# Expert 2 and the output biases are loaded without waiting for the first gather, and the row limit of the indirect DMAs sits in one register

## The reference

```python
x = x + tanh(g_xattn) * (gelu(layernorm(x) @ ctx.T) @ ctx)          # per batch, ctx is 375 x 256
xf = layernorm(x).reshape(896, 256)
top1 = argmax(xf @ gate_w.T + gate_b)                                # 8 experts
y[t] = relu(xf[t] @ w1[top1[t]].T + b1[top1[t]]) @ w2[top1[t]].T + b2[top1[t]]
x = x + tanh(g_ffn) * y
```

## Time and profile before

| | us |
|---|---|
| median of 3 runs | 105.25 |
| lowest, highest | 104.97, 105.46 |
| the profiled execution | 105.14 |
| its span in the trace | 103.3 |
| PE busy | 95.3 (92%) |
| DVE, ACT, POOL busy | 51.8, 35.8, 39.6 |
| granted clock of PE, mean | 0.99 |

### The profile page before, as it was taken

How to read it: one execution, slowest core, us unless ns; L and a number is a source line. 1 busy time by engine, 2 the same in 40 slices (tenths; PEclk the granted TensorE clock), 3 DMA queues, 4 the chain that set the end, 5 groups by cost and what they waited for, 6 DMA issues and landing times.

```text
span 103.3 us, 2099 instructions
## 1 busy us (share of the span) xinstructions
PE 95.3 (92%) x676; PEld 88.2 (85%) x677; DVE 51.8 (50%) x203; ACT 35.8 (35%) x104; POOL 39.6 (38%) x96
## 2 busy tenths in 40 slices
PE   5999999999999799999999999999999999999700
PEld 5989988789978689999998898998998999988500
DVE  0643796767799758299584432350540431233100
ACT  5716458666684126333431140230230330400000
POOL 3448778333947507771025025730300300300330
PEclk9999999999999999999999999999999999999997
DMA  2999999999999501599999999999999310100110
GB/s 61 231 394 407 401 403 436 399 424 420 406 403 421 191 10 31 117 362 336 318 423 411 407 416 435 399 412 421 425 419 423 136 46 0 39 3 6 51 52 4
DMA packets 7086, 28.66 MB, mean 277 GB/s; under 512 B 1181, under 2 KB 2591, under 8 KB 5024
## 3 DMA queue, kind: packets, MB, share of 16 engines
q1 hardware_dynamic: 5040, 25.40, 61.7%
q0 software_dynamic: 864, 2.12, 6.7%
q10 hardware_dynamic: 1168, 0.98, 2.8%
HBM read 26.64 MB, written 2.11 MB: 278 GB/s over the span
## 4 chain that ended last, share of the span: by engine, by line
PE 85%; DVE 8%; issue 2%; POOL 1%; ACT 0%; POOLq 0%; DVEq 0%
PE bank L1069 24%; PE bank L1078 23%; PE bank L977 9%; PE bank L989 8%; PE bank L1085 5%; PE bank L1022 4%; PE bank L1032 4%; PE bank L967 2%; PE bank L1010 2%; PE bank L1056 1%; DVE x L642 1%; DVE stats L649 1%; POOL out_rows L403 1%; DVE cand L673 1%; DVE lg L663 1%
## 5 line engine op out<-in xcount | busy, mean ns | idle before, releaser
L1069 PE MATMUL bank<-region,w 128*128 128x128 f32 x224 | 26.4, 276 | 0.0
L1069 PEld LDWEIGHTS bank<-region,w 128*128 128x128 f32 x224 | 26.0, 192 | 0.4 <-issue 0.2
L1078 PE MATMUL bank<-w,region 128*128 128x256 f32 x112 | 25.2, 379 | 0.0
L1078 PEld LDWEIGHTS bank<-w,region 128*128 128x128 f32 x112 | 20.8, 190 | 2.6
L403 POOL DMA_INDIRECT out_rows<-region,to_row x9 | 8.9, 989 | 28.7 <-DVE region L879 26.8
L578 ACT ACTIVATE region<-bank,smalls 128x128 f32<-128x128 f32 x28 | 8.7, 363 | 30.7 <-PE bank L1069 30.7
L398 POOL DMA_INDIRECT region<-x_rows,from_row x9 | 9.3, 1031 | 17.9 <-DMA region<-x_rows,from_row 12.2
L863 DVE TENSOR_SCALAR region<-bank,smalls 128x128 f32<-128x128 f32 x28 | 8.4, 346 | 13.7 <-PE bank L1069 12.2
L977 PEld LDWEIGHTS bank<-w,region 128*128 128x128 f32 x96 | 11.7, 192 | 1.2 <-issue 0.4
L977 PE MATMUL bank<-w,region 128*128 128x120 f32 x96 | 12.1, 276 | 0.2 <-issue 0.2
L879 DVE SCALAR_TENSOR_TENSOR region<-bank,tg,region 128x256 f32<-128x256 f32 (+1 forms) x8 | 3.9, 484 | 16.6 <-PE bank L1078 16.6
(11 more groups left out here) (149 smaller groups left out, 109.4 us busy)
## 6 DMA issues: line engine op xcount, KB each, us to landing
w<-in_w1t SPq DMA_DIRECT2D x8, 1024.0 KB, 13.5
w<-in_w2t SPq DMA_DIRECT2D x8, 1024.0 KB, 15.9
region<-in_ctx SPq DMA_DIRECT2D x3, 792.0 KB, 14.1
region<-in_ctx SPq DMA_DIRECT2D x5, 408.0 KB, 8.3
region<-in_ctx SPq DMA_DIRECT2D x5, 384.0 KB, 6.9
x_rows<-x ACTq DMA_DIRECT2D x8, 113.8 KB, 6.7
b2b<-in_b SPq DMA_DIRECT2D x1, 896.0 KB, 12.1
x<-in_x_rest SPq DMA_DIRECT2D x1, 670.0 KB, 6.4
```

What stands on the lines that cost most here:

```text
L1069: mm = pe.matmul(hT_ps[k][:, part % 2 * P:(part % 2 + 1) * P], w1[:, e, n * H + part * P:n * H + (part + 1) * P], xgT[:, j % 2, n * P:(n + ...
L1078: mm = pe.matmul(y[:, 0:D], hidT[:, q, part, :], w2[:, e, part * D:(part + 1) * D], start=(part == 0), stop=(part == KH - 1))
```

## The change

```diff
             load_expert(0)
             sp.dma_start(b2b[:, 0:D], b2[0:D].partition_broadcast(P)).then_inc(b2_in[0], 16)
             load_expert(1)
-
-            sp.wait_ge(xnT_done, B)
-            sp.wait_ge(xgT_done, 1)
-            sp.wait_ge(first_in[1], 16)
+            sp.dma_start(b2b[:, D:E * D], b2[D:E * D].partition_broadcast(P)).then_inc(b2_in[1], 16)
+
+            sp.wait_ge(w1_in[1], 16)
             load_expert(2)
-            sp.dma_start(b2b[:, D:E * D], b2[D:E * D].partition_broadcast(P)).then_inc(b2_in[1], 16)
             for e in range(3, E):
                 sp.wait_ge(xgT_done, e - 1)
...
             def gather(to, idx):
                 return pool.indirect_dma_start(
                     out=to, out_offset=None, in_=x2_dram, in_offset=bass.IndirectOffsetOnAxis(ap=idx, axis=0),
-                    bounds_check=TOKENS - 1, oob_is_err=False)
+                    bounds_check=last_row, oob_is_err=False)
 
             def scatter(rows, idx):
                 return pool.indirect_dma_start(
                     out=out, out_offset=bass.IndirectOffsetOnAxis(ap=idx, axis=0), in_=rows, in_offset=None,
-                    bounds_check=TOKENS - 1, oob_is_err=False)
-
+                    bounds_check=last_row, oob_is_err=False)
+
+            last_row = pool.snap(pool.to_reg(TOKENS - 1))
             pool.wait_ge(x2_stored, 16 * B)
             pool.wait_ge(rows0_ok, 1)
```

## The result

The changed kernel takes 106.66 us (median of 4, 106.30 to 107.02) against 105.35 (median of 4) for the kernel before in the same comparison: ratio 1.013, 95% interval 1.009 to 1.016. It is slower, by 1.3 us. Its profiled execution took 106.30 us with a span of 104.1, so 1.16 us more than the 105.14 of before.

The account below looks back on a forecast made before the run. The prediction took PE to bound the kernel, the chain from 34.7 to 97.5 us. A stall of +1.1 us and a tail of -0.5 gave +0.6: 105.74 from the profiled 105.14, stated as 105.8 us, range 104.9 to 107.1.

Parts of the forecast that it names:

- (A): Rival at POOL's indirect DMAs: the wait doesn't shorten, PE stalls 1.5 us, tail gains 0.03; 106.6 us, chance 0.28.
- the prediction's own signs of being wrong: Last store landing at 40 us or sooner, gather well over 4 us, or PE idle somewhere behind 50 us.
- PE had nothing to gain: PE's matmuls: after 37.2 us PE waits for nothing, so an earlier load can't bring anything.
- The last store at 41.0: Last store, sharing with loads: bounds 40.2 and 41.3 us for its landing, the later end favoured, 41.0 taken.
- (B): Rival at the first gather: it lands at 43.6, PE doesn't stall, tail 0.5 us shorter; 104.6 us, chance 0.22.
- The first gather lands at 45.4 and PE stalls 1.1 us: First gather starts at 41.3, lands at 45.4 against 44.3 allowed, so PE stalls 1.1 us ahead of turn_block(1).
- the 1.0 us for the loads that it still meets: First gather: 1.0 us added to its 3.1 us in the empty hole, for the loads still running.
- The second gate adds nothing: Second gather, through DVE to pair 1 of up(2): 0.3 us beyond its slack, inside the 1.1 us already lost.
- I cost it at nothing: Expert 3's gather, for the turn at 54.25 us: now second, not fourth, in a queue meeting loads; cost nothing.
- The tail shorter by 0.5 us: Last scatter behind finish: POOL's moved wait saves 0.5 us, between bounds of 0.03 and 0.54.
- The bound from the DMA rates: SP's load queue at 0.37 MB/us: 3.42 MB ends at about 42.2 us, last engines at about 44.4.
- (C): Rival at the early gathers: loads keep both at 7.0 us, PE stalls 4.0 us; 108.6 us, chance 0.07.

Follow-up runs that it names:

- gather3_first: The full change, with expert 3's gather third instead of fifth in POOL's queue and its normalisation earlier; ratio 1.002 to the kernel before.
- w1_ahead: POOL's part, plus the biases and w1 of expert 2 (1.9 MB) ahead of SP's pause, w2 behind it; ratio 1.014 to the kernel before.
- POOL's part alone: The kernel before with only POOL's diff, SP keeping its pause; ratio 1.012, and 0.994 (105.04 us) when run again on another chip.
- bias_ahead: POOL's part, plus only the 896 KB of biases moved ahead of SP's pause; ratio 0.995 to the kernel before.
- SP's part alone: The kernel before with only SP's diff, POOL still writing the row limit ahead of each indirect DMA; ratio 1.016, 107.46 us.

## Why the prediction was right, and where its terms were off

The sign held, and so did the two mechanisms: late gathers make PE wait, and the tail is shorter. The size is in part luck. +0.6 us was forecast and +1.3 measured, inside the range but twice the forecast, and nearer to the 106.6 of rival (A), which the traces rule out. In the trace the stalls and the tail do add up to +0.6, but from other terms than those forecast. Two of the prediction's own signs of being wrong appeared: PE waits behind 50 us, at `up(2)` and at the turn of expert 3.

**PE had nothing to gain.** Off by up to 0.4 us. It was read from a trace in which w1 of expert 3 landed 0.1 us before PE wanted it. The second trace of the kernel before has PE waiting for it, and the change removes that wait. The gain is smaller than what the late gathers cost.

**The last store at 41.0.** It landed at 33.76 + 7.51 = 41.27. The choice of the later bound was right: the store's issue was 0.5 us later in this trace, but its 7.5 us to landing are more than the 6.9 of the row. Where it was issued at 33.36 to 33.39, as in the kernel before, it landed at 41.0 and 41.1 (`gather3_first`, `w1_ahead`). (B) needed a landing before 40.4 and is out.

**The first gather lands at 45.4 and PE stalls 1.1 us.** The start was right (41.57 against 41.3). The term that was mis-sized is the 1.0 us for the loads that it still meets: it took 3.2 us from start to landing, 0.1 more than in the empty hole, since its packets came when the loads had run out (w2 of expert 2 landed at 44.0, and from 43.0 to 44.8 us the DMA view has 0.02 MB on SP's queue and 0.13 on POOL's). The stall at `turn_block(1)` was 0.26 us. In the traces of `w1_ahead` and `gather3_first`, where attention ended earlier and the last store was issued earlier too, PE is idle 0.30 and 0.20 us there, so the small stall isn't a matter of one trace.

**The second gate adds nothing.** Its size was right (0.3 forecast, 0.22 measured), but with a smaller first stall it did add.

**"I cost it at nothing": expert 3's gather.** This step failed. I counted places in the queue and expected that meeting the loads as the second gather would make up for the later start. (Before, expert 3's was the fifth gather and not the fourth, and the third to meet loads.) The loads of expert 3 were issued at 45.7, together with the spill rows' gather, and from there on gathers took 8.0 us each, hardly less than the 7.8 and 8.3 of before. So the later start, 47.10 against 44.51, came through almost whole: expert 3's rows landed 2.2 us later (55.06 against about 52.8). Against that stood 0.8 us of slack and the delay that PE already had. PE lost 0.61 us there, and the experiment with its gather in third place took this wait away. So the 1.1 us of stall came out as a sum (1.09) of three parts, of which I had put all into the first. That it agrees is luck: one term was 0.8 us too large, another was missing.

**The tail shorter by 0.5 us.** 0.52 in the trace. (A) is out: all eleven traces with the wait on the DMA itself show 0.28 us, the three with a waiting MOVE 0.80. The rule of the Trainium skill ("Perfetto Trace Analysis", "DMA Instruction — SWDGE (GPSIMD)") that a software DMA waits in a queue behind its decoding fits these numbers.

**The bound from the DMA rates.** The loads did end near 44 us as said (w2 of expert 2, issued at 34.12, landed 9.9 us later), and (C) with both early gathers at 7 us didn't come about (3.2 and 3.0).

## What to carry to other kernels

A hole in the transfers isn't waste if short dependent transfers run through it. Here stores of 114 KB took 7.5 instead of 3.7 us and gathers 7 to 8 instead of 3 when loads ran beside them, and PE, which needed none of the loads put there any earlier, waited for them. Before filling such a hole find what passes through it and its slack, and follow every later transfer of that queue, not the first alone: here the late start of the first gather was passed on to the fifth, where it cost most. What may go in is what delays the last store by less than that slack: here 0.9 MB of biases were free and 1.9 MB cost as much as 3 MB. And look in a second trace before you call a load in time: here w1 of expert 3 was in time by 0.1 us in the first trace, and PE waited for it in the second.

If an engine's DMA has to wait, let the DMA hold the wait and put the registers that it needs ahead of it. In the traces it saved 0.5 us in the tail and 0.6 at the first gather.

## What the runs showed that was not expected

In three traces of one comparison, on one chip, PE's signals reached ACT and SP late. ACT's copy of a turned block starts 0.41 to 0.48 us behind the beginning of the turn elsewhere; it started 1.57 us behind it in POOL's part alone (expert 1), 1.04 in `bias_ahead` (expert 1), and 1.34 and 1.56 in SP's part alone (the second and the fifth turn). SP's next load, which waits for the same signal, was late each time as well. The matmuls behind started 0.8 and 0.3 us late in the first two. A fourth trace of that comparison and the ten others have nothing of the kind, one of them the same kernel on another chip. Whether the chip, the moment or a matmul that in truth ended late makes it isn't settled, and it can't be from these records. It is a warning on single comparisons here: one kernel gave 1.012 (1.005 to 1.019) in one and 0.994 (0.990 to 0.998) in the next, each with an interval that excludes the other.

The sequencer of POOL shows about 0.5 us for each indirect DMA instruction (0.51 us behind the MOVE of the last scatter), ahead of the 1.0 us of the DMA's record on the engine. Between two gathers in a row this is hidden, where 0.30 us lie between the records; behind a MOVE that waits it is not.
